# Head 0 of a cross attention: keys loaded straight into the stacked layout and split there, and the first token tile normed and split ahead of the second

## The reference

```python
x = x + _L0_xattn_ref(_layernorm(x, axis=-1), ctx_2048)

def _L0_xattn_ref(qkv, y):            # N_HEADS = 16
    bs, width, length = qkv.shape     # 1, 256, 512
    ch = width // N_HEADS             # 16
    q = qkv.reshape(bs * N_HEADS, ch, length)
    k = v = y.reshape(bs * N_HEADS, ch, -1)        # 16 x (16, 8192)
    scale = 1.0 / math.sqrt(math.sqrt(ch))
    weight = jnp.einsum('bct,bcs->bts', q * scale, k * scale)
    weight = jax.nn.softmax(weight.astype(jnp.float32), axis=-1)
    a = jnp.einsum('bts,bcs->bct', weight, v)
    return a.reshape(bs, -1, length)
```

## Time and profile before

| | |
|---|---|
| median of 3 runs | 1383.09 us (1382.91 to 1384.27) |
| the profiled execution's own time | 1384.99 us |
| its span in the profile | 1383.2 us |
| TensorE busy | 1342.5 us, 97% of the span |
| VectorE / ScalarE / GpSimd busy | 1098.8 / 970.4 / 156.6 us |
| DMA | 199.51 MB, mean 144 GB/s |

### The profile page before, as it was taken

One profiled execution on the slowest core, in us unless ns is written; L12 is line 12 of the kernel. 1 busy time (PEld: TensorE's weight loads), 2 busy tenths in 40 slices (PEclk: granted clock), 3 DMA queues, 4 the chain that ended last, 5 costly groups with the idle time before them and its releaser, 6 DMA issues. The chain is left out here.

```text
span 1383.2 us, 28377 instructions
## 1 busy us (share of the span) xinstructions
PE 1342.5 (97%) x10645; PEld 884.7 (64%) x10645; DVE 1098.8 (79%) x2195; ACT 970.4 (70%) x1892; POOL 156.6 (11%) x216
## 2 busy tenths in 40 slices
PE   3999999999999999999999999999999999999999
PEld 2544444444444444444458999999988864568998
DVE  5999989999999999997867666666668667887665
ACT  1499989999999999999474555555535632785553
POOL 4122222122222222120000000000000000000000
PEclk9999999999999999999999999999999999999999
DMA  7566556665566655456204755555528524204651
GB/s 189 125 142 143 108 166 170 161 162 131 113 138 143 134 117 130 108 90 86 92 1 150 298 187 187 189 188 187 192 87 358 244 86 158 70 1 126 184 190 39
DMA packets 75338, 199.51 MB, mean 144 GB/s; under 512 B 35512, under 2 KB 43616, under 8 KB 63040
## 3 DMA queue, kind: packets, MB, share of 16 engines
q1 hardware_dynamic: 75024, 197.69, 50.2%
q10 hardware_dynamic: 192, 0.20, 0.1%
HBM read 170.64 MB, written 23.80 MB: 141 GB/s over the span
## 5 line engine op out<-in xcount | busy, mean ns | idle before, releaser
L754 ACT ACTIVATE probs<-bank 128x512 f32<-128x512 f32 x1024 | 541.1, 617 | 50.7 <-PE bank L812 48.4
L672 DVE TENSOR_REDUCE pm<-bank 128x1 f32<-128x512 f32 x736 | 466.3, 682 | 47.4 <-PE bank L793 46.8
L812 PE MATMUL bank<-qst,kst 52*128 52x512 f32 (+1 forms) x1024 | 336.4, 437 | 5.2 <-DMA qst<-nscratch 5.2
L793 PE MATMUL bank<-kst,qst 48*128 48x512 f32 x904 | 316.0, 451 | 21.2 <-DMA qst<-qsplit 20.2
L824 PE MATMUL bank<-probs,vext 128*32 128x256 f32 (+3 forms) x4024 | 295.2, 394 | 0.6
L812 PEld LDWEIGHTS bank<-qst,kst 52*128 52x128 f32 (+1 forms) x1024 | 163.3, 187 | 193.8 <-DVE pm L672 94.2
L1591 PE MATMUL bank<-e_xhi,e_hi 128*128 128x256 f32 (+1 forms) x768 | 217.4, 283 | 0.3 <-DVE e_xlo L283 0.2
L1591 PE MATMUL bank<-e_xhi,e_lo 128*128 128x256 f32 (+1 forms) x768 | 217.3, 283 | 0.0
L1591 PE MATMUL bank<-e_xlo,e_hi 128*128 128x256 f32 (+1 forms) x768 | 217.2, 283 | 0.0
L824 PEld LDWEIGHTS bank<-probs,vext 128*32 128x32 f32 x4024 | 92.4, 109 | 118.2 <-issue 103.6
L793 PEld LDWEIGHTS bank<-kst,qst 48*128 48x128 f32 x904 | 140.7, 188 | 30.8 <-DMA qst<-qsplit 20.2
(11 more groups left out here) (251 smaller groups left out, 1770.8 us busy)
## 6 DMA issues: line engine op xcount, KB each, us to landing
raw<-wall SPq DMA_DIRECT2D x43, 1536.0 KB, 6.5
kst<-kscratch SPq DMA_DIRECT2D x192, 128.0 KB, 4.5
kscratch<-ksplit SPq DMA_DIRECT2D x15, 1024.0 KB, 4.3
kraw<-ctx_rows SPq DMA_DIRECT2D x16, 512.0 KB, 6.2
vraw<-ctx_vt SPq DMA_DIRECT2D x16, 512.0 KB, 6.2
ctxT<-ctxT SPq DMA_DIRECT2D x8, 1024.0 KB, 9.5
nat<-ctx_chunks SPq DMA_DIRECT2D x6, 1024.0 KB, 20.0
weights<-wscratch SPq DMA_DIRECT2D x16, 256.0 KB, 3.6
```

What stands on the lines that cost most here:

```text
L672: nc.vector.tensor_reduce(max_at(p, 1), bank[:, pre_bank(p), :], AX.X, ALU.max).then_inc(pre_reduced, 1)
L754: nc.scalar.activation(probs[:, (XST * k + n) % PR, :], bank[:, score_bank(XST * k + n), :], ACT.Exp, scale=XSCALE).then_inc(probs_ready, 1)
L793: ins = nc.tensor.matmul(bank[:, pre_bank(p), :], qst[64 * j:64 * j + KR, h, tt * P:tt * P + P], keys, start=True, stop=True)
L812: nc.tensor.matmul(bank[:, score_bank(s), :], kst[64 * j:64 * j + rows, h % 2, m * P:m * P + P], qst[64 * j:64 * j + rows, h, :], start=Tr ...
```

## The change

- Head 0's keys no longer go through the cast, the scratch and the twelve loads. `load_first(half)` issues two DMAs (j = 0, 1), each of which reads 16 rows of 2048 keys four times over (a broadcast of 4 in front of the 16 rows) into 64 partitions of `first_raw`, 512 KB each, so that a half is 1 MB.
- The split is done in that layout. `low_row` is 1 on the partitions of the low rows and 0 elsewhere (one VectorE reduction of the identity). `first_high` = raw times `low_row`, rounded; `kst` = raw minus `first_high`, rounded, which is the low part on the low rows and the high part on the others. In half 0 POOL does columns 0 to 1023 and VectorE 1024 to 2047 (a multiply and a subtraction each); in half 1 POOL does all 2048 columns.
- SP's order becomes: X tile 0, `load_first(0)`, X tile 1, a wait for the keys of half 0 and for the six query DMAs (`stack_lo[0]` at 96), `load_first(1)`, then the keys and pairs of head 1. The loop is the same but for one more wait ahead of the marks.
- POOL's order becomes: identity, marks, `first_low` of half 0, `first_low` of half 1, then `split(1)` and the rest as before.
- VectorE norms and splits token tile 0 alone (the per-tile helpers of the later layers), then does its part of half 0's keys, then token tile 1. ScalarE's root of tile 1 stands behind its six query DMAs.
- TensorE's first matmul waits for half 0's split and the queries, its 33rd (k = 1) for half 1's split.

```diff
+FIRST_LOADS = 2 * 16
+FIRST_KEYS = [3, 5]
...
 def raw_loads(h):
-    return 16 if h == 0 else 80 * (h // 2 + h % 2) + 16 * (1 - h % 2)
+    return 80 * (h // 2 + h % 2) + FIRST_LOADS * NS * (1 - h % 2)
 def cuts(h):
-    return 2 if h == 0 else 5 * h - 1
+    return 5 * h + 2
...
+            def load_first(half):
+                keys = ctx_rows[0].rearrange("(c s) n -> c (s n)", c=XC)
+                for j in range(2):
+                    lo = j * XK + half * XK // 2
+                    sp.dma_start(first_raw[64 * j:64 * j + 64, half, :],
+                                 keys[:, lo:lo + XK // 2].unsqueeze(0).to_broadcast([4, XC, XK // 2])).then_inc(kraw_loaded[0], 16)
-            sp.dma_start(X[:, :, :], x.rearrange("(a p) d -> p a d", p=P)).then_inc(x_loaded, 16)
-            load_raw(0)
+            sp.dma_start(X[:, 0, :], x[0:P]).then_inc(x_loaded[0], 16)
+            load_first(0)
+            sp.dma_start(X[:, 1, :], x[P:]).then_inc(x_loaded[1], 16)
+            sp.wait_ge(kraw_loaded[0], FIRST_LOADS)
+            sp.wait_ge(stack_lo[0], 96)
+            load_first(1)
             load_raw(1)
             load_pairs(1)
-            sp.wait_ge(split_step, 1)
-            sp.dma_start(kscratch[0, 0], ksplit[:, 0, :].bitcast(F32)).then_inc(first_high_stored, 16)
-            sp.wait_ge(split_step, 2)
-            sp.dma_start(kscratch[0, 1], ksplit[:, 1, :].bitcast(F32)).then_inc(split_stored, 16)
-            sp.wait_ge(first_high_stored, 16)
-            load_rows(0, 0, K_ROWS[0])
-            load_rows(0, 0, K_ROWS[2])
-            sp.wait_ge(split_stored, 16)
-            load_rows(0, 0, K_ROWS[1])
-            sp.wait_ge(stack_lo[0], 192)
-            load_stack(0, 1)
             sp.wait_ge(qsplit_ready, 4)
...
                 if h == 0:
                     load_v(0)
                     sp.wait_ge(const_set, 2)
+                    sp.wait_ge(split_step, FIRST_KEYS[1])
...
+            def first_low(half, lo, hi):
+                pool.wait_ge(kraw_loaded[0], FIRST_LOADS * (half + 1))
+                if half:
+                    pool.wait_ge(split_step, FIRST_KEYS[0])
+                nc.gpsimd.tensor_scalar(first_high[:, half, lo:hi], first_raw[:, half, lo:hi], low_row[:, :], None,
+                                        ALU.mult).then_inc(split_step, 1)
+                pool.wait_ge(split_step, [1, FIRST_KEYS[0] + 1][half])
+                nc.gpsimd.tensor_tensor(kst[:, 0, XK // 2 * half + lo:XK // 2 * half + hi], first_raw[:, half, lo:hi],
+                                        first_high[:, half, lo:hi].bitcast(F32), ALU.subtract).then_inc(split_step, 1)
-            split(0)
+            nc.gpsimd.memset(marks[:, :, :].bitcast(F32), 1.0).then_inc(const_set, 1)
+            pool.wait_ge(const_set, 1)
+            nc.gpsimd.memset(marks[0:2, 1, :].bitcast(F32), 0.0).then_inc(const_set, 1)
+            pool.wait_ge(dve_step.sem, 1)
+            first_low(0, 0, XK // 4)
+            first_low(1, 0, XK // 2)
             pool.wait_ge(qsplit_ready, 4)
             split(1)
             split_apart(1)
-            nc.gpsimd.memset(marks[:, :, :].bitcast(F32), 1.0).then_inc(const_set, 1)
-            pool.wait_ge(const_set, 1)
-            nc.gpsimd.memset(marks[0:2, 1, :].bitcast(F32), 0.0).then_inc(const_set, 1)
...
-            dve.wait_ge(x_loaded, 16)
-            norm_dve(g, dve, link)
+            dve.wait_ge(g.ident_ready, 2)
+            link(nc.vector.tensor_reduce(low_row[:, :], ident[:, :].rearrange("p (j r c) -> p r j c", j=2, c=XC)[:, 1], AX.XY, ALU.add))
             for a in range(TA):
+                dve.wait_ge(x_loaded[a], 16)
+                tile_spread(g, 0, a, link)
+                tile_scale(g, dve, 0, a, link)
                 dve.wait_ge(g.xn_ready, a + 1)
                 nc.vector.tensor_copy(qsplit[:, 0, a], xn[:, a, :]).then_inc(qsplit_ready, 1)
                 dve.wait_ge(qsplit_ready, 2 * a + 1)
                 nc.vector.tensor_tensor(qsplit[:, 1, a], xn[:, a, :], qsplit[:, 0, a].bitcast(F32), ALU.subtract).then_inc(qsplit_ready, 1)
+                if a == 0:
+                    dve.wait_ge(kraw_loaded[0], FIRST_LOADS)
+                    link(nc.vector.tensor_scalar(first_high[:, 0, XK // 4:], first_raw[:, 0, XK // 4:], low_row[:, :], None, ALU.mult))
+                    dve.wait_ge(split_step, 1)
+                    nc.vector.tensor_tensor(kst[:, 0, XK // 4:XK // 2], first_raw[:, 0, XK // 4:], first_high[:, 0, XK // 4:].bitcast(F32),
+                                            ALU.subtract).then_inc(split_step, 1)
...
-            act.wait_ge(kraw_loaded[0], 16)
-            nc.scalar.copy(ksplit[:, 0, :], kraw[:, 0, :]).then_inc(split_step, 1)
-            act.wait_ge(g.var_ready, 1)
-            nc.scalar.activation(g.std[:, :, :], g.var[:, :, :], ACT.Sqrt).then_inc(g.std_ready, 1)
+            tile_root(g, act, 0, 0)
             for row, part in Q_ROWS:
...
+            tile_root(g, act, 0, 1)
...
                 if r == 0:
-                    pe.wait_ge([stack_lo, stack_hi][half][h % 2], stacked(h, half))
+                    if h == 0:
+                        pe.wait_ge(split_step, FIRST_KEYS[half])
+                    if k != 1:
+                        pe.wait_ge([stack_lo, stack_hi][half][h % 2], stacked(h, half))
```

More of the change, by code:

```diff
@@ L88, in raw_loads @@
 def raw_loads(h):
-    return 16 if h == 0 else 80 * (h // 2 + h % 2) + 16 * (1 - h % 2)
+    return 80 * (h // 2 + h % 2) + FIRST_LOADS * NS * (1 - h % 2)
 def cuts(h):
-    return 2 if h == 0 else 5 * h - 1
+    return 5 * h + 2
 def stacked(h, half):
-    return [192, 96][half] * (h // 2 + 1) + 48 * (h // 2 + h % 2)
+    return [192, 96][half] * (h // 2 + 1) + 48 * (h // 2 + h % 2) - 96 * (1 - h % 2)
 def score_bank(s):
@@ L189, in setup @@
     return g
-def norm_dve(g, dve, link):
-    nc = g.nc
-    for a in range(TA):
-        ins = nc.vector.bn_stats(g.stats[:, a, :], g.X[:, a, :])
-    link(ins)
-    for a in range(TA):
-        ins = nc.vector.bn_aggr(g.mv[:, a, :], g.stats[:, a, :])
-    link(ins)
-    nc.vector.tensor_scalar(g.var[:, :, :], g.mv[:, :, 1:2], EPS, None, ALU.add).then_inc(g.var_ready, 1)
-    dve.wait_ge(g.std_ready, 1)
-    link(nc.vector.reciprocal(g.rstd[:, :, :], g.std[:, :, :]))
-    for a in range(TA):
-        ins = nc.vector.tensor_scalar(g.std[:, a, :], g.rstd[:, a, :], g.rstd[:, a, :], None, ALU.mult)
-    link(ins)
-    for a in range(TA):
-        ins = nc.vector.tensor_scalar(g.std[:, a, :], g.std[:, a, :], -0.5, g.var[:, a, :], ALU.mult, ALU.mult)
-    link(ins)
-    for a in range(TA):
-        ins = nc.vector.tensor_scalar(g.rstd[:, a, :], g.std[:, a, :], 1.5, g.rstd[:, a, :], ALU.add, ALU.mult)
-    link(ins)
-    for a in range(TA):
-        nc.vector.tensor_scalar(g.xn[:, a, :], g.X[:, a, :], g.mv[:, a, 0:1], g.rstd[:, a, :],
-                                ALU.subtract, ALU.mult).then_inc(g.xn_ready, 1)
 def roots(k, a):
-    return TA * k + a
+    return TA * k + a + 1
 def turned_bank(k, a):
@@ L334, in cross_attention_0 @@
     marks = at(0, "marks", [4, 2, XK // 2], F32R)
+    first_raw = at(96, "first_raw", [P, NS, XK // 2])
+    first_high = at(16, "first_high", [P, NS, XK // 2], F32R)
+    low_row = at(174.875, "low_row", [P, 1])
     nscratch = nc.dram_tensor("nscratch", [XN, P, 32], F32, kind="Internal").ap()
@@ L339, in cross_attention_0 @@
     oscratch = nc.dram_tensor("oscratch", [XH, P, D], F32, kind="Internal").ap()
-    x_loaded = sem("x_loaded")
+    x_loaded = [sem("x_loaded0"), sem("x_loaded1")]
     kraw_loaded = [sem("kraw_loaded0"), sem("kraw_loaded1")]
@@ L344, in cross_attention_0 @@
     split_stored = sem("split_stored")
-    first_high_stored = sem("first_high_stored")
     stack_lo = [sem("stack_lo0"), sem("stack_lo1")]
@@ L436, in load_stack @@
                 if half == 0:
-                    sp.wait_ge(split_stored, 32 * h + 16)
+                    sp.wait_ge(split_stored, 32 * h)
                 if h >= 2:
@@ L564, in split @@
                 pool.wait_ge(kraw_loaded[h % 2], raw_loads(h))
-                if h > 0:
-                    pool.wait_ge(split_stored, 32 * h - 16)
-                    if h == 1:
-                        pool.wait_ge(first_high_stored, 16)
-                    nc.gpsimd.tensor_copy(ksplit[:, 0, :], kraw[:, h % 2, :]).then_inc(split_step, 1)
+                if h > 1:
+                    pool.wait_ge(split_stored, 32 * (h - 1))
+                nc.gpsimd.tensor_copy(ksplit[:, 0, :], kraw[:, h % 2, :]).then_inc(split_step, 1)
                 pool.wait_ge(split_step, cuts(h) - 1)
@@ L631, in _ @@
                 if h == XH - 1:
-                    pool.wait_ge(split_stored, 32 * XH - 16)
+                    pool.wait_ge(split_stored, 32 * (XH - 1))
                     pool.wait_ge(nsplit_step, 2 * NS * h + 2)
```

## The result

The changed kernel took 1416.60 us (median of 4 runs, 1416.18 to 1419.15) beside 1383.68 us (4 runs) of the kernel before: a ratio of 1.0227 on record, 95% interval 1.0209 to 1.0245 (the two medians alone give 1.0238). It is slower, as forecast, but by 32.9 us where 10.5 were forecast, and far above the range. The profiled execution took 1416.18 us, its span is 1414.4 us, 31.2 us more than before.

A forecast was written before the change was run, and what follows sets the result against it. The prediction took SP's reaching `stack_negmax(0)`, which sets the first score, as the bound: +10.0 us there and +0.5 us for the clock gave +10.5 us, 1393.6 us. The range was 1381.5 to 1397 us.

The forecast's parts named there:

- the SP chain to `stack_negmax(0)`: SP's queue before the first score: ends last of two chains; `stack_negmax(0)` at 52.5 us in place of 42.54, +10.0 us.
- VectorE's pairs: VectorE's pair reductions for the maxima: run from 20 to 48 us, not late against a first score at 58 us.
- Rival A: Half 1's key load uses all engines: keys at 18 to 20.5 us, +4.2 us, 1387.3 us; chance 0.25.
- B: Rival on SP's queue: it drains at its issue rate; with all engines −4.0 us, 1379.1 us; chance 0.12.
- C: Rival, no change: POOL's extra work eaten by the saved backlog, all engines used, +/- 2 us, 1383 us; chance 0.10.
- the rate of the new load: Half 1's key load: 4 engines at 26 GB/s, 104 GB/s, 10.1 us for 1 MB; keys there at 25.6 us.
- rival D: Key load at the marks' own 42 GB/s: 25 us for a half, some +25 us; chance 0.03.
- POOL's multiply: POOL's split of half 1's 2048 columns: multiply at the cast's rate, 2 x 1.04 us; split 6.9 us with gaps.
- the backlog: SP from `store_apart(1)` to `stack_negmax(0)`: some 4 us of 19.2 were queued key pieces, now gone, leaving 15.2 us.
- The clock's 0.5 us: After TensorE's idle time of about 9 us before the first score: longer slow-clock stretch, +0.5 us, within 0 and 1.5.
- TensorE's start: First matmul at some 16 to 17 us, well before 20; a real gain of 4 to 6 us for TensorE's start.

The follow-up runs named there:

- e1: The changed kernel with each copy of the 16 key rows a DMA of its own, eight a half instead of two; 1398.79 us, ratio 1.0100.
- e3: The changed kernel with the same two DMAs a half reading 64 different rows, no broadcast (head 0's keys wrong); 1399.62 us, one run.
- e2: The changed kernel with a broadcast of 2 in front instead of 4, four DMAs of 32 rows a half; 1423.84 us, one run.
- e6: e1 with POOL's two multiplies of the key split given to ScalarE; 1397.11 us, ratio 1.0072.
- e5: e1 with head 1 ahead of half 1 on POOL and SP, and the marks behind head 1's loads; 1388.87 us, ratio 1.0009.
- e8: e1 with the second buffer's two marks DMAs issued right behind head 1's loads; 1395.81 us, ratio 1.0060.
- e9: e1 with e5's order, e6's multiplies, and the second buffer's marks right behind the values; 1383.35 us, ratio 0.9998.
- e11: e9 with POOL's split of head 1 held until VectorE split tile 1, and head 1's loads behind the queries; 1384.48 us, ratio 1.0007.
- e12: The kernel before with head 1's six query loads issued behind the store of the maxima; 1387.16 us, ratio 1.0019.

## Why the prediction was wrong in size

**What held.** The bound was read rightly: the SP chain to `stack_negmax(0)` sets the first score, and the end follows it. Over all fourteen kernels the first score moves from 47.1 to 87.4 us and the remainder only from 1331.8 to 1338.7. The queries were issued early: the cast of tile 0 ended at 7.6 us (forecast 8.1) and their DMAs were issued in 3.81 us. The load did use four engines. The path half 1's keys, POOL, `store_apart(1)`, marks, maxima was the right one, TensorE did stand still for 9.5 us (forecast 9), and VectorE's pairs were not late: the 24 were done at 71.8 us and not at 48, but SP was later still. Rival A's and B's first condition, all engines, is refuted in the changed kernel, and C's with it.

**The step that failed: the rate of the new load.** The prediction said "4 engines at 26 GB/s, 104 GB/s". The four move 69 to 75 GB/s together, and 50 to 52 over the whole of a half, with other DMAs beside them. The 8 us too little counts twice, because SP may issue half 1 only when half 0 has landed: half 0 landed at 22.0 and not near 13, so half 1 was issued 8.5 us late and took 8.0 us more: 16.5 us. I had taken the engines' count from the nearest row, the marks, and their speed from another, the 128-row load. The marks' own 42 GB/s stood beside it and was given 0.03 as rival D. The range should have reached that end. Its price was short as well: 25 us for each half puts half 1's keys at some 51 us, 25 later than the forecast had them, so some +36 us over before and not +25. That the broadcast inside the DMA is the cause is shown by e1 and e3; that an engine moves less with four copies than with two is shown by e2; why it does is not settled. The same traffic kept the queries from landing at 13.5 us: the slowest of the six, issued between 7.7 and 10.9 us, took 10.4 us. That cost nothing more, since half 0's keys came later still.

**A term mis-sized: POOL's multiply.** "At the cast's rate" was 2.1 us; it took 5.45. A multiply by a scalar that differs by partition is not a cast, and no row of before had one on POOL. With the subtraction, 10.0 us in place of 6.9: 3.1 us. Shown by e6.

**A saving that was not there: the backlog.** The 19.2 us from `store_apart(1)` to `stack_negmax(0)` were to shrink by 4; they measured 18.5, 3.3 over the forecast 15.2. The marks are what the queue waits for (e5: 2.63 us for the six loads without them; e8: 4.9 us less with two marks fewer). The prediction had both readings and used each once: it kept the 8.54 us of the key loads "since the marks drain in front of them", and took the 4 us off all the same. The marks and these loads together took 12.9 us from the first issue to the end of the last (58.69 to 71.61), and 13.9 before (24.91 to 38.76).

The three add to 22.9 us at `stack_negmax(0)` (75.40 less 52.5). From there to the first score it was 5.0 us, not 6.0, so the first score is 21.9 us over the forecast 58.5. The clock's 0.5 us did not show: the remainder is 0.7 us shorter than before, which is within what two executions differ by. One reading under it does not hold either: the prediction called TensorE slow at the start by its weight loads, but the granted clock from 22 to 26 us stands as 1.00 in the earlier trace rows.

TensorE's start was wrong too, 29.0 us for 16 to 17, by the same load and by VectorE's subtraction of 3.40 us. It cost nothing: the maxima of half 0 were turned at 63.9 us, and SP came for them at 75.40.

A slip in the chances: by the prediction's own parts slower has 0.71 (0.50, 0.18 and 0.03) and the same 0.17 (0.10 and 0.07), not 0.70 and 0.18.

**What undoing each part gives.** In first scores: the broadcast 18.6 us (80.44 to 61.84, e1); from there the order on POOL and SP 9.9 (to 51.97, e5), or the multiply alone 3.2 (e6), which overlap; order, multiplies and marks together 14.5 (to 47.39, e9). The idea's own gain, TensorE's earlier start, is then real but does not arrive: in e9 the first matmul starts at 16.50 us (20.19 before), but the first pair at 21.51 (21.03 before), behind the norm of tile 1. In e11 the pair starts at 18.44, and the marks hold up the maxima.

Not tried: the copies behind the 16 rows in one DMA; marks written by the split itself; the four copies on partitions that are not 32 apart. Whether a kernel without the marks' DMAs would gain from the early queries stays open.

## What to carry to other kernels

Where a queue of loads feeds a late, small transfer, ask of each new load how its source lies outermost: the broadcast in front made this load take twice as long as the same bytes in e1 (20.1 us for 9.7), and a load that waits for its predecessor counts the error twice. Take count and speed of a resource from the same row, and if the nearest row is slow, let the range reach it. Moving work to an idle engine costs what is queued behind it there, not its busy share.

## What the runs showed of the hardware

- A load with a broadcast of c copies outermost used c engines: share 0.25 for four, 0.13 for two; 64 plain rows had 0.98. Two moved 26 GB/s each, four 17 to 19. The same bytes went at 141 to 154 GB/s in 16-row DMAs and at 206 to 227 in 64-row ones.
- POOL's multiply by a per-partition scalar: 5.45 us for 2048 columns, and 3.31 for 1024 with a wait of some 0.6 us for VectorE in it; its cast of 1024 took 1.04. ScalarE did the 2048 in 2.00, VectorE 1024 in 0.75.
- VectorE and POOL hold each other up, and the one that starts second pays: VectorE's subtraction 3.40 us for 1.23 when POOL's started 0.02 us ahead, POOL's 3.35 for 2.34 when VectorE's started 0.08 us ahead (e6); a cast of VectorE's 2.45 for 0.41.
- Four 16 KB rows into neighbouring partitions hold up issues on both queues: six key loads 6.90 us for 2.63, six query DMAs of ScalarE 8.39 for 3.80, and the load that follows a small store comes after 5.6 us for 2.3.
- After TensorE stood still, the clock came back after very different times: 6.9 us in the profiled execution before, 17.1 in e12, 20.9 from the first score in e3. With it low for all 17.1 us of a stretch in e12, ScalarE did 7 activations fewer than in the kernel before, where it was low for 6.9 of them. Executions of one kernel differ too, by their mean granted clock (0.989 to 1.000 before). That decides a few microseconds, and no edit was found that sets it.
